# An early-fusion transformer block on one core: normalisation, gate, bias, stack loads, rectification and low parts as single steps in the written-out order

## The reference

```
p = patches(x)                       # 64 x 784 patches of 3*8*8
h = p @ W_embed + b_embed + pos
for i in range(3):                   # graph of the 28x28 grid, both directions
    hw = h @ W_gcn[i]
    h = relu(A_norm @ hw + b_gcn[i]) # written as a scatter-add over edges
h = h @ W_out + b_out                # 64 x 784 x 64
tok = concat(h, txt)                 # 64 x 861 x 64
tok = tok + attention(layernorm(tok))   # 4 heads of 16, softmax over 861 keys
y = layernorm(tok)
out = tok + shared_mlp(y) + sum_e gate_e(y) * expert_e(y)
```

## Time and profile before

| | |
|---|---|
| median of 3 runs | 5771.88 us |
| lowest and highest | 5768.51, 5806.13 us |
| the profiled execution | 5753.58 us |
| its span | 5751.5 us |
| mean granted PE clock | 0.906 |

### The profile page before, as it was taken

The page is one execution under the profiler, slowest core; times in us unless marked ns, Lnnn a source line. Parts: engine busy times, 40 slices in busy tenths (PEclk is TensorE's granted clock), DMA queues, the critical chain, the costliest instruction groups (busy, mean ns, idle before and its releaser), DMA issues.

```text
span 5751.5 us, 86873 instructions
## 1 busy us (share of the span) xinstructions
PE 5221.1 (91%) x29710; PEld 3413.1 (59%) x29710; DVE 3560.4 (62%) x7660; ACT 3017.6 (52%) x6161; POOL 1237.4 (22%) x1169
## 2 busy tenths in 40 slices
PE   4489999999989999999998999999998999999997
PEld 3356666566666556666655666556665556666654
DVE  2256666666656666666665666666665666666664
ACT  0045555555555555555554555555555555555555
POOL 1112222221221221222221222222122122122112
PEclk8589999899989989999988999899999999999988
DMA  1444244334334434334424334433433433443320
GB/s 36 66 72 69 49 69 71 57 60 73 59 56 75 64 55 68 64 52 72 73 54 61 63 54 71 69 60 58 72 60 56 75 62 57 68 65 52 54 41 5
DMA packets 331178, 347.28 MB, mean 60 GB/s; under 512 B 108778, under 2 KB 280938, under 8 KB 330730
## 3 DMA queue, kind: packets, MB, share of 16 engines
q1 hardware_dynamic: 289770, 228.36, 20.8%
q10 hardware_dynamic: 40960, 113.28, 16.1%
HBM read 269.85 MB, written 70.73 MB: 59 GB/s over the span
## 4 chain that ended last, share of the span: by engine, by line
PE 57%; DVE 18%; DMA 10%; issue 5%; ACT 3%; ACTq 2%; SPq 1%; POOL 0%; DVEq 0%; POOLq 0%
PE ps L1028 10%; PE ps L1040 10%; PE ps L1019 9%; PE ps L1076 8%; DVE neg_max_halves L835 8%; DMA k_stack<-qk_scratch 8%; PE ps L1094 4%; PE ps L1067 3%; PE ps L1158 3%; PE ps L1137 3%; ACT probs L722 1%; PE ps L1082 1%; DVE hidden L985 1%; PE ps L1052 1%; PE ps L1135 1%
## 5 line engine op out<-in xcount | busy, mean ns | idle before, releaser
L835 DVE TENSOR_REDUCE neg_max_halves<-ps 123x1 f32<-123x432 f32 (+1 forms) x3584 | 2003.6, 599 | 949.5 <-PE ps L1040 936.6
L722 ACT ACTIVATE probs<-ps 123x432 f32<-123x432 f32 x3584 | 1710.5, 536 | 749.7 <-PE ps L1019 615.5
L1040 PE MATMUL ps<-k_stack,q_stack 96*123 96x432 f32 x3584 | 1341.7, 415 | 159.7 <-DMA k_stack<-qk_scratch 59.2
L1019 PE MATMUL ps<-q_stack,k_stack 97*123 97x432 f32 x3584 | 1376.3, 435 | 88.4 <-DVE neg_max_halves L835 28.8
L1040 PEld LDWEIGHTS ps<-k_stack,q_stack 96*123 96x123 f32 x3584 | 672.7, 195 | 632.1 <-issue 360.6
L1019 PEld LDWEIGHTS ps<-q_stack,k_stack 97*123 97x123 f32 x3584 | 713.5, 207 | 446.3 <-DVE neg_max_halves L835 135.7
L1028 PE MATMUL ps<-probs,v_and_one 123*32 123x432 f32 x7168 | 823.6, 576 | 11.4 <-ACT probs L722 11.4
L1076 PE MATMUL ps<-adjacency,parts_hi 112*128 112x392 f32 x1344 | 472.9, 352 | 17.7 <-ACT probs L722 12.9
L793 ACT ACTIVATE hidden<-ps,plain_w 128x432 f32<-128x432 f32 x640 | 398.8, 632 | 128.0 <-PE ps L1094 127.7
L1076 PE MATMUL ps<-adjacency,parts_lo 112*128 112x392 f32 x1344 | 462.0, 344 | 0.0
L1028 PEld LDWEIGHTS ps<-probs,v_and_one 123*32 123x32 f32 x7168 | 184.7, 115 | 429.9 <-issue 285.0
(11 more groups left out here) (156 smaller groups left out, 6359.0 us busy)
## 6 DMA issues: line engine op xcount, KB each, us to landing
q_stack<-qk_scratch ACTq DMA_DIRECT2D x256, 216.0 KB, 9.5
k_stack<-qk_scratch ACTq DMA_DIRECT2D x256, 216.0 KB, 10.7
image_rows<-in_x SPq DMA_DIRECT2D x768, 49.0 KB
image_rows<-in_x SPq DMA_DIRECT2D x768, 48.8 KB
image_rows<-in_x SPq DMA_DIRECT2D x768, 48.6 KB
image_rows<-in_x SPq DMA_DIRECT2D x768, 48.3 KB
qk_scratch<-parts_hi SPq DMA_DIRECT2D x64, 432.0 KB, 2.5
qk_scratch<-parts_lo SPq DMA_DIRECT2D x64, 432.0 KB, 3.8
```

Of the source, the lines that this page charges most:

```text
L722: act.activation(P[:, (g * 2 * NB + unit) % SLOTS, h, :], T[0:BLK, 0:HW], ACT.Exp, scale=SCALE).then_inc(free[r], 1)
L835: v.tensor_reduce(NM[:, qb * HEADS + h, half:half + 1], T[0:BLK, 0:keys], AX.X, ALU.max, negate=True).then_inc(free[r], 1)
L1019: mm = pe.matmul(T[0:BLK, 0:cn], KS[:, g % 2, h, kb * BLK:(kb + 1) * BLK], QS[:, g % 2, h, c0:c0 + cn], start=True, stop=True)
L1040: mm = pe.matmul(T[0:BLK, 0:cn], QS[0:SHIFT_ROW, g % 2, h, qb * BLK:(qb + 1) * BLK], KS[0:SHIFT_ROW, g % 2, h, c0:c0 + cn], start=True, st ...
```

## The change

No instruction on data is added or dropped. What was one step with several instructions becomes several steps, each with its own time in the list, so that steps of other parts, maxima above all, stand between them:

- a normalisation was three steps and is nine (sum, mean, ln, sq on ACT, var, ln2, scale, hi, lo);
- the gate's g2 and g3 were steps among the experts; after "gate" there are now 20 steps with times of their own (GATE), where each waits only for the one it reads (`done` and `need` in place of `settle`);
- the bias is nine steps of POOL with times of their own (BIAS). Its first waits for the output projection and the centring instead of the gate's weights;
- the eight stack loads are eight steps with times of their own (STACK); they stood together at g - 1.0;
- the joining of maxima ("nm") and "mrow" stand one or two maxima behind the last of theirs;
- relu, the low parts of the graph ("gwl") and of the queries and keys ("qkl") and the copy-out of sums ("oev") stand a little behind the matmul or copy they follow;
- the table of times is new.

```diff
-            if h == 1 and n and n % 2 == 0:
-                out.append(sum_pair(g, units, n - 2))
-    return out + [sum_pair(g, units, 2 * NB - 2)]
...
+            if h == 1:
+                out += due
+                due = []
+                if n and n % 2 == 0:
+                    out.append([("pv", g, *one) for one in units[n - 2:n]])
+                    due = [("oev", g, half) for half, kb in units[n - 2:n] if kb == NB - 1]
...
+                out.append(("mx", g, qb, h, half))
+                out += due[:1] if half else []
+                due = due[1:] if half else due
+        due += {3: [("nm", g, 0), ("mrow", g, 0)], NB - 1: [("nm", g, 1), ("mrow", g, 1)]}.get(qb, [])
+    return out + [due[0], ("wait", 0.2), due[1]]
...
-    return [(k, g, which) for k in ("ln", "ln2", "ln3")]
+    for k in ("sum", "mean", "ln", "wait", "sq", "wait", "var", "ln2", "wait", "scale", "hi", "lo"):
+        out.append(("wait", 0.1) if k == "wait" else (k, g, which))
...
+GATE_CHAIN = ("gmax", "gsub", "wait", "gexp", "wait", "gsum", "grec", "gprob", "gcmp", "gexp2", "gtie", "gadd", "grank",
+              "gsel", "gsum2", "grec2", "gweight", "part0", "rest0", "part1", "rest1", "part2")
...
-        out += {0: [("g2", g)], 1: [("g3", g)], 2: [[("l2", g, 0, 0), ("l2", g, 0, 1)], ("hb", g)], 3: [],
-                4: [[("l2", g, 1, 0), ("l2", g, 1, 1)]]}[e]
+        out += {2: [[("l2", g, 0, 0), ("l2", g, 0, 1)]], 4: [[("l2", g, 1, 0), ("l2", g, 1, 1)]]}.get(e, [])
...
-MAX = ((-0.768, 0.045), (-0.751, 0.05))
...
-NORM_M = ((1.131, 1.265), (1.15, 1.254))
...
-PROJECT = ((-1.265, -1.106), (-1.399, -1.257))
...
+MAX = ((-0.693, 0.164), (-0.666, 0.131))
+FINISH = ((0.995, 1.084), (1.072, 1.165))
+NORM_M = ((1.093, 1.222), (1.167, 1.195))
+EXPERT = ((1.369, 1.997), (1.264, 1.87))
+GATE = ((1.467, 1.649), (1.347, 1.492))
+BIAS = ((1.661, 1.802), (1.55, 1.73))
+NORM_A = ((-1.483, -1.351), (-1.672, -1.474))
+PROJECT = ((-1.277, -1.241), (-1.361, -1.296))
+STACK = ((-1.08, -1.016), (-1.082, -0.936))
...
-        + [(g - 1.0, ("stack", g)), (g + VALUE[b], ("v", g))]
...
-                        g = st[1]
-                        counted(pool, g_weight, nth, ("g3", g))
-                        emptied(pool, turn, ("back", g - 1))
+                        _, g, n = st
...
+                        if n == 0:
+                            emptied(pool, turn, ("wo", g))
+                            counted(pool, centred, nth, ("ln", g, "m"))
+                            ins = pool.tensor_tensor(hb, hb, row("sb3").unsqueeze(1).to_broadcast(shape), ALU.add)
+                        elif n % 2:
+                            counted(pool, g_weight, nth, ("gweight", g))
...
-                        counted(act, scratch_dma, nth, ("scratch", g), 32)
-                        filled(act, turn, ("s", g - 2, 1, NB - 1, HEADS - 1))
-                        for part in range(2):
...
+                        if n == 0:
+                            counted(act, scratch_dma, nth, ("scratch", g), 32)
+                            filled(act, turn, ("s", g - 2, 1, NB - 1, HEADS - 1))
...
+                        elif kind == "rest0":
+                            need(("part0", g))
+                            done(v.tensor_tensor(GR[:, 0, :, :], GW[:, :, :], GP[:, :, 0, :], ALU.subtract), st)
```

More of the change, by code:

```diff
@@ L78 @@
 UNROLL = 8
+STACK_PARTS = 8
 SLOTS = 3
@@ L703, in run @@
                 scratch_last = latest(steps, "scratch")
+                hb_no = ranks(steps, lambda st: st[0] == "hb" and st[2] == 2 * EXPERTS)
                 pv_no = ranks(steps, lambda st: st[0] == "pv" and st[3] < NB - 1)
@@ L809, in _, with done, need, settle @@
         def _(v):
-            chain = [0]
-            def settle(ins):
+            chain, made = [0], {}
+            def done(ins, st):
                 chain[0] += 1
                 ins.then_inc(v_chain, 1)
-                v.wait_ge(v_chain, chain[0])
+                made[st] = chain[0]
+            def need(st):
+                if st in made:
+                    v.wait_ge(v_chain, made[st])
+            def settle(ins):
+                done(ins, "last")
+                need("last")
             def run(steps, base, init):
                 chain[0] = 0
+                made.clear()
                 turn, nth = turns(steps), ordinal(steps)
```

304 lines of the change are left out of this document (180 added, 124 removed).

## The result

The changed kernel takes 5851.03 us (median of 4 runs, 5838.22 to 5856.55), the kernel before 5778.55 us beside it (5768.51 to 5806.13). The ratio is 1.0127, 95% interval 1.0093 to 1.0161: slower by 1.3%. The forecast was 5553 us and faster, with a range that ended at 5785 us. It was wrong.

A forecast was written before the change was run, and what follows sets the result against it. PE, busy 91% but paced by hand-overs, with DVE the local limit at the gate: 5753.6 - 116 - 16 - 117 - 30 + 60 = 5534.6, plus 18.3 to the median, 5553 us; 8-in-10 range 5400 to 5785.

The forecast's parts named there:

- New waits: Steps queued before late givers, such as DVE before scaling in the odd image's normalisation: costs 60 us, bounds 0 and 95.
- rival B: On SP, the row of maxima meets the stack loads and reaches the scores late: slower, 5873 us, chance 0.10.
- Gate and normalisation: DVE's runs cut into single steps between maxima, so PE stops less for banks: gain 116 us, bounds 0 and 193.3.
- the five rows: PE's waits for banks freed late by DVE, 193.3 us together; predicted to fall under 80 us.
- Row of maxima: PE's 21.2 us wait for the negated maxima before their transposition, now behind further maxima: gain 16 us.
- Stack loads: ACT's eight stack loads as single, earlier steps: gain 117 us, k_stack wait inside it, bounds nothing and 177.
- Relu and low parts: These and the copy-outs as own steps, so ACT does not stop before DVE: taken as 0, between 0 and 30 us.
- Clock: With fewer PE stops the lower clock level is granted less often: gain 30 us.
- 0.93 or more: Sign that the forecast is right: PE's clock in the steady stretch rises to this, from 0.92.
- L1059 stays near 1.0 us: Sign: DVE's gate subtraction, L976 before at 1009 ns, keeps its length because it shares ports with POOL.
- Rival D: POOL's bias steps and DVE block each other, 141 us more DVE time: 5694 us, chance 0.08.
- Rival C: Much better: PE's bank, maxima and stack-load losses and a fourth of the clock's go: 5341 us, chance 0.14.

The follow-up runs named there:

- a_pack_late: Changed kernel with the first load's packing and embedding behind POOL's second scaling, and the second load and its packing moved back: 5314.94 us, 0.9232.
- t_times_only: Kernel before with no step taken apart, only the change's values in its table of times: 6036.18 us, 1.0469.
- p_bursts_l1: Changed kernel, packing late, third-quarter load ahead of the maxima on SP, steps together again except the bias, gate's new place kept: 6037.19 us, 1.0492.
- p_gate_bursts: On a_pack_late, the gate's 20 steps put together again as four runs: 5459.04 us, 0.9494.
- a_max_old: Changed kernel with the maxima's times (MAX) as before and the third-quarter load kept ahead of its row of maxima: 5680.95 us, 0.9847.
- a_load_first: Changed kernel with the first image load of each pair ahead of the row of maxima on SP: 5516.11 us, 0.9588.
- b_load_late: Kernel before with the first image load of each pair 0.12 of an image later, where it meets the stack loads: 6116.3 us, 1.062.

## Why the prediction was wrong

**The step that failed** is the term *New waits*: 60 us, bounded at 95. It looked for late givers only at the normalisation, and took one pow on POOL for each image as the most that could happen. The sum says that "what changes is the position of every small step and the table of times", but the sum never follows what the moves do to the order on SP and POOL (only rival B looks at SP). Measured are 30 waits of 15.8 us, 474.1 us in all, for POOL's scaling behind a packing that waits for a late image load; with that packing out of the way (a_pack_late) the row is 27.3 us and the time 5315 us, below the forecast. The second step without a term is the table of times: the sum counts it only where it frees k_stack.

The runs can be put in a row, in ratios to the kernel before. It is one of several possible orders, and another would share out the parts differently:

| | ratio | step |
|---|---|---|
| the times alone (t_times_only) | 1.0469 | +0.047, +270 us |
| and SP's order, packing late, the gate's place, bias single (p_bursts_l1) | 1.0492 | +0.002 |
| and all other steps single (a_pack_late) | 0.9232 | -0.126, -726 us |
| and packing and loads as the change has them (the changed kernel) | 1.0127 | +0.090, +515 us |

The forecast had a gain of 219 us in all, nearly all of it for what stands in the third row.

- *Gate and normalisation, 116 us.* Mechanism right: the five rows went from 193.3 to 60.3 us. Size wrong: 144 and 157 us, each taken alone. A burst costs more than its PE wait, since it also lowers the clock: in p_gate_bursts 74 of 153 us are busy time of PE. The bound (193.3, the waits only) was itself too low.
- *Row of maxima, 16 us.* The wait for neg_max went from 21.2 to 1.3 us, and the two steps are worth 131 us where SP's order is kept. But the place of "mrow" sets when SP's next load fires, and that I did not look at.
- *Stack loads, 117 us.* Right: 98 us measured, k_stack only at the start, the exponentials behind issues 3.9 us. (By the list the last of the eight stands 0.331 and 0.288 of an image ahead of the first maximum, not 0.323 and 0.27; the sum doesn't use it.) What I missed is that loads begun earlier meet the image load.
- *Relu and low parts, 0.* "They carry the same instructions" was the wrong argument. Put near, they are worth 44 us (bound 30). And relu as a step took POOL's scaling behind the packing; with the late load that is the wait of 474 us. No run of the changed kernel put relu alone back.
- *Clock, 30 us.* The steady clock is 0.91, not 0.93 or more; in a_pack_late it is 0.97. The long stops explain a part at most, since a_max_old is without them and at 0.912 over its span. And the mean clock was a poor sign to watch: it fell by 0.01 in the steady window, while over the span the low clock within PE's busy time went from 917 to 522 us.
- *New waits, 60 us.* The term that failed: bounded by a pow of 1.5 us at normalisations, where the real wait is 15.8 us long, for another step of POOL, and comes from SP's queue.
- *L1059 stays near 1.0 us*: wrong, as the group of the changed kernel shows, where it was 1009 ns:

```profile
L1059 DVE TENSOR_TENSOR gate_weight_rest<-gate_weights,gate_weight_parts 123x28 f32<-123x28 f32 x64 | 38.7, 605 | 1.1
```

- *Rival B* forecast 5873 us, near the 5851 measured, but that is luck. It had the right queue and the wrong step: it asked whether SP's row writes come too late for the scores when they meet the stack loads; the step behind them, the load, was late first. Its own wait does exist: 154.9 us in a_load_first. *Rival D* did not come: DVE's total fell by 112 us. *Rival C* (5341 us) lies near what the change gives once the collision is out (5315), though the parts are others than its terms: single steps worth 722 us together against times that cost 270.

## What to carry to other kernels

When a list of times moves a step, write down for each queue that takes its work in turn (SP's and POOL's too) which neighbours it now has, what each of them waits for, and what is queued behind; a transfer behind a step that waits for late data fires with that data. Give a step that waits for a transfer a place behind everything urgent on its engine, so that a late transfer costs little (27.3 us of PE's time here, not 474.1). And measure a new order and its times together: here one swap on SP decided 433 us, and single steps were worth 722 us with the collision out (6037 to 5315) while with it the changed kernel is only 185 us below t_times_only (6036 to 5851). When you read a clock, look at how much of the low level falls on busy time.

## What the runs showed that I had not expected

- The same 24 loads of image rows are there 16.3 us after their first issue in a_max_old (begun at 4507.83, packed from 4524.10 on), where the first stack load is issued 10.8 us after them, and 35.4 us after it in the changed kernel, where 1.7 MB of stack loads (8 of 216 KB) begin 2.9 us later:

```profile
4507.83 9.41 SPq L603 DMA_DIRECT2D image_rows<-in_x  x24
...
4524.10 1.80 POOL L692 COPY patch_columns<-image_rows 96x392 f32<-96x392 f32 x2 [5.16 <-DMA image_rows<-in_x]
```

- Issues slow down beside transfers of another queue. SP's four row writes take 3.02 us in a_load_first although they stand right behind SP's own 24 image loads, which are still under way (lines above; the stack loads begin later there). In a_max_old they take 11.61 us while ACT's stack loads are in flight and the image rows have landed:

```profile
4529.32 11.61 SPq L619 DMA_DIRECT2D q_stack<-image_rows  x4
```

- The same in a_pack_late: 3.02 us when the DMA engines are idle (share 0.01 in the first window below), and 17.34 us beginning 9.3 us after the last stack load was issued. The engines were 0.93 busy in the 13 us before it (second window) and 0.45 during it. And in b_load_late, where the eight stack loads are issued within 3.7 us around its start, the issue of 24 image loads takes 26.63 us, where it takes 9.83 in the kernel before.

```profile
4350.67 3.02 SPq L619 DMA_DIRECT2D q_stack<-image_rows  x4
...
4376.93 17.34 SPq L619 DMA_DIRECT2D q_stack<-image_rows  x4
```

```profile
4350.00:4354.00 4.00, 4.00 (x19) 1.95 (x18) 1.27 (x3) 1.60 (x3) 0.00 (x0) 1.00 0.01 2
4364.00:4377.00 13.00, 13.00 (x99) 11.01 (x97) 6.67 (x16) 7.22 (x15) 2.04 (x2) 1.00 0.93 93
```

- The subtraction L1059 takes 605 ns on average where it took 1009 before, with the same 28 elements. It still runs beside a step of POOL, all 64 times in both kernels, and ends within 51 ns behind that step's end: 42 to 51 ns before, 41 to 48 ns in the changed kernel. What changed is how long POOL's step has been running when the subtraction begins: 0.17 to 0.20 us before, 0.17 to 0.57 us now. In a_pack_late it begins 19 times while POOL is idle, and takes 170 to 180 ns. So what sets its length here is what is left of POOL's step, and not its 28 elements. DVE still waits that out in every image; my forecast of 1.0 us failed because it took POOL's step to be as far along as before.
